# A graph layer and its experts: node gathers 1.5 batches earlier in POOL's order, the expert program a batch earlier

## The chip, the cores and the metric

The kernel runs on one core of a Trainium2 chip. The metric is device time in microseconds, the median over runs. Matmuls run on TensorE (PE), elementwise work on VectorE (DVE) and ScalarE (ACT), indirect DMAs (gathers) are issued by GpSimd (POOL), plain DMAs by SyncE (SP). Each engine works through its own instructions in order; semaphores join them.

## The reference

```python
def gat_conv(x, W, attn_l, attn_r, src, dst, n_nodes):      # twice, over the edges src -> dst
    feat = (x @ W).reshape(n_nodes, H, D)
    e = leaky_relu(el[src] + er[dst], 0.2)                  # el, er: feat dotted with attn_l, attn_r
    ex = exp(e - segment_max(e, dst)[dst])
    alpha = ex / segment_sum(ex, dst)[dst]
    return segment_sum(alpha * feat[src], dst)
...
xn = _layernorm(x, axis=-1)
x = x + gnn(xn) + linear_attention(xn)                      # 6250 nodes, 256 features, 106250 edges
h = _layernorm(x, axis=-1)
w = softmax(h @ Wr + br)                                    # 8 experts, every node through all
y = sum_e w[:, e] * (relu(bn(relu(bn(h @ W1[e])) @ W2[e])) @ Wo[e] + bo[e])
out = x + y
```

## The kernel before

Layer two of the graph network and the experts run in one pass (`edge_pass` with `Experts`). The edges, sorted by their target node, are cut into 13 groups (Q) of 4 batches (PB); a batch n has 16 steps j (G). At each step POOL gathers 128 rows of the table (L1349), ACT scales them (L1486) and DVE adds them to a running sum along each of 128 lanes, the ring (L1463). Three buffers (B) hold the rows, so POOL may be up to three batches ahead of DVE; it waits for `summed` of the batch three back. At step 6 of a batch DVE does the `head` of the next one (L1402 to L1421), which waits for all 16 gathers of that next batch. SP stores the sums of each half batch.

A node whose edges run over lanes or groups needs carries, the tails. For group q they are made in the first batch of the group after it (n = 4q + 4): ACT copies the last sums, then TensorE and DVE turn, scan (DVE step 3), shift (step 6), scale (step 8) and join (step 12, ending with L1191). SP then writes them to memory (`sync_out`, L1248 and L1250), with `tails.out` as their semaphore.

When group g is complete, its nodes (4 blocks of 121) go through the expert program. POOL gathers for each block its sums and its carries: 8 node gathers (`gather`, L1829), the first of which waits for the stores and for `tails.out`. In the order before they stand behind the first 8 edge gathers of batch 4(g + 2), one after each. DVE merges the two parts (`below`, `shares`, `join`), adds the residual, takes mean and variance (`spread`) and normalizes (`norm`, L1952 and L1955); TensorE transposes (`turn`, L2137), ACT copies (`turned`), TensorE forms the gate logits (`gate`, L2148) and runs the 8 experts: `first_layer` (L2097), `second_layer` (L2109), `outputs` (L2123), with ACT's `keep` (L2032) between them and DVE's `add_result` (L1885) behind. The order on each engine is written out by hand: on DVE, ACT and SP by batch and step (r = n // 4, kq = n % 4; f = r - 2 is the group whose experts run, g = r - 1 the one that is joined), on TensorE by the loop in `tensor` over r and the expert e, two experts for a batch. Batches beyond the 52nd exist only for the expert program (`vector_last`, `scalar_last`, `sync_last`), and the node gathers of the last two groups stand in `pool_last`.

Of the kernel before, what the change touches and what calls it, by code (L numbers as in the profile page):

```python
# [19 lines left out]
G = 16  # L20
T = NB * G
Q = 13
PB = NB // Q
J = T // Q
CAP = P * J
KB = NB // Q
# [3 lines left out]
E = 8  # L30
# [17 lines left out]
class Layer:  # L48


    def __init__(self, name, heads, width, act_heads, buffers, ahead):
        self.name, self.heads, self.width = name, heads, width
        self.buffers, self.ahead = buffers, ahead
        self.dim = width // heads
        self.table = width + 8
        self.row = width + 2 * heads
        self.den = width
        self.max = width + heads
        self.act_heads = act_heads
# [736 lines left out]
class Mixing:  # L796
# [263 lines left out]
    def pool(self, pool, n, j):  # L1060
        pass
# [636 lines left out]
class Experts:  # L1698
# [3 lines left out]


    LAST = (Q + 2) * PB

    def __init__(self, nc, a, k, s, tails, stored):
        self.nc, self.a, self.k, self.tails, self.stored = nc, a, k, tails, stored
# [57 lines left out]
    def valid(self, f):  # L1765
        return 0 <= f < Q


    def sync_first(self, sp):
        a = self.a  # L1770
# [30 lines left out]
                     self.y[:, f % 3, :, :]).then_inc(self.y_out, 16)  # L1801

    def sync(self, sp, n, half):
        r, kq = n // PB, n % PB
        if kq == 1 and half == 0 and self.valid(r - 3):
            self.store(sp, r - 3)
        if kq == 1 and half == 1 and self.valid(r - 1):
            self.load_rest(sp, r - 1)

    def sync_last(self, sp):  # L1810
        for n in range(NB, self.LAST + 3):
            self.sync(sp, n, 0)
# [19 lines left out]
                                     ).then_inc(self.rows_in[i], 16)  # L1832

    def pool(self, pool, n, j):
        if n % PB == 0 and n >= 2 * PB and j < 2 * KB:
            self.gather(pool, n // PB - 2, j // 2, j % 2)

    def pool_last(self, pool):
        for g in (Q - 2, Q - 1):
            for i in range(KB):  # L1840
                for j in range(2):
                    self.gather(pool, g, i, j)
# [140 lines left out]
        nc.vector.tensor_tensor(self.w[:, :, :], self.lge[:, :, :], broad(self.tot[:, :], E), ALU.mult).then_inc(self.w_ready, 1)  # L1983

    def vector(self, dve, n, j):
        r, kq = n // PB, n % PB
        f, g = r - 2, r - 1
        if j in (1, 2, 8, 9):
            o, e = (f, 2 * kq - 2) if kq else (r - 3, E - 2)
            if self.valid(o):  # L1990
                self.add_result(dve, o, e if j < 8 else e + 1, (j - 1) % 7)
        if self.valid(f):
            if kq == 0 and j == 3:
                self.gates(dve, f)
            if kq == 0 and j == 12:
                self.gate_shares(dve, f)
            if kq == 3 and j in (3, 4):
                self.add_bias(dve, f, j - 3)
        if not self.valid(g):
            return  # L2000
        if kq == 2:
            if j == 3:
                self.below(dve, g)
            if j == 7:
                self.shares(dve, g)
            if j in (7, 10, 11, 13):
                self.join(dve, g, (7, 10, 11, 13).index(j))
            if j == 14:
                self.spread(dve, g)
        if kq == 3 and j == 5:  # L2010
            self.norm(dve, g)

    def vector_last(self, dve):
        for n in range(NB, self.LAST + 3):
            for j in range(1, G):
# [33 lines left out]
        last.then_inc(self.xt_ready, 1)  # L2049

    def scalar(self, act, n, j):
        nc, r, kq = self.nc, n // PB, n % PB
        f, g = r - 2, r - 1
        if self.valid(f):
            if j == 2:
                self.keep(act, f, 2 * kq + 1, 0)
            if j == 5:
                self.keep(act, f, 2 * kq, 1)
            if kq == 0 and j == 7:
                act.wait_ge(self.lg_ready, f + 1)  # L2060
                wait(act, self.w_ready, f)
                nc.scalar.activation(self.lge[:, :, :], self.lg[:, :, :], ACT.Exp).then_inc(self.lge_ready, 1)
            if kq == 2 and j == 3:
                self.weights(act, f)
        if self.valid(g):
            if kq == 2 and j == 4:
                act.wait_ge(self.d_ready, g + 1)
                wait(act, self.joined, KB * g)
                nc.scalar.activation(self.sc[:, :, :], self.d[:, :, :], ACT.Exp).then_inc(self.sc_ready, 1)
            if kq == 3 and j == 3:  # L2070
                act.wait_ge(self.sd_asked, g + 1)
                nc.scalar.activation(self.sd[:, :], self.var[:, :], ACT.Sqrt).then_inc(self.sd_done, 1)
            if kq == 3 and j == 8:
                self.turned(act, g, 0)
                self.turned(act, g, 1)
        if self.valid(f):
            if kq < 3 and j == 9:
                self.keep(act, f, 2 * kq + 2, 0)
            if j == (12 if kq < 3 else 10):
                self.keep(act, f, 2 * kq + 1, 1)  # L2080
        if self.valid(g) and kq == 3 and j == 13:
            self.keep(act, g, 0, 0)

    def scalar_last(self, act):
        for n in range(NB, self.LAST + 3):
            for j in range(G):
# [81 lines left out]
    def tensor(self, pe):  # L2168
        tails = self.tails
        for r in range(Q + 3):  # L2170
            f, g, o, q = r - 2, r - 1, r - 3, r - 1
            on = self.valid(f)
            for e in range(E):
                if e == 7 and self.valid(g):
                    self.turn(pe, g)
                if on and e < E - 1:
                    self.first_layer(pe, f, e + 1)
                if e == 0 and self.valid(q):
                    tails.tensor_turn(pe, q)
                if e == 1 and self.valid(q):  # L2180
                    if on:
                        pe.wait_ge(self.lg_ready, f + 1)
                    tails.tensor_sum(pe, q)
                if e == 2 and 0 <= q < Q - 1:
                    tails.tensor_spread(pe, q)
                if e == 4 and on:
                    self.turn_weights(pe, f)
                if e == 5 and on:
                    self.bias(pe, f)
                if on:  # L2190
                    self.second_layer(pe, f, e)
                if e == 0 and self.valid(q):
                    tails.tensor_back(pe, q)
                if e == 7 and self.valid(g):
                    pe.wait_ge(self.xt_ready, 2 * (g + 1))
                    if g == 0:
                        for i in range(4):
                            pe.wait_ge(self.f1_in[i], 16)
                    self.first_layer(pe, g, 0)
                if e == 0 and self.valid(o):  # L2200
                    self.outputs(pe, o, E - 1)
                if e > 0 and on:
                    self.outputs(pe, f, e - 1)
                if e == 7 and self.valid(g):
                    self.gate(pe, g)


# [82 lines left out]
```

## Time and profile before

| | us |
|---|---|
| median of 3 runs (lowest, highest) | 3355.85 (3355.46, 3357.4) |
| the profiled execution's own time | 3355.96 |
| its span, first to last instruction | 3353.5 |
| layer two's first edge gather on POOL | 1925.7 |
| its last edge gather on POOL | 3122.65 |

The span is the profiled execution without the 2.5 us that lie around it; times of instructions are microseconds from the start of the span. "Idle before" in a row is the time in which the engine did nothing ahead of the row, with what released it; "issue" is a releaser that the profile doesn't show.

### The profile page before, as it was taken

What the parts mean: (1) busy time and instruction counts of PE and PEld (TensorE: products, weight loads), DVE (VectorE), ACT (ScalarE), POOL (GpSimd) and SP (SyncE); (2) the same over time, 40 slices, a digit from 0 to 9 for tenths busy, and PEclk for the clock granted to TensorE, in tenths of its full rate; (3) what the DMA queues carried; (4) which work ended last, traced back from release to release, by engine and by line L of the source; (5) the groups of instructions that cost most, each with busy time, mean ns of one, the idle gap of its engine ahead of it and who ended that gap; (6) DMA issues with size and microseconds to landing.
All of it is one profiled execution on the core that took longest, in us unless ns stands there. A gap on an engine that the chain in (4) does not pass through costs nothing. (4 is left out here: it accounts for less than half of the span.)

```text
span 3353.5 us, 33809 instructions
## 1 busy us (share of the span) xinstructions
PE 2061.7 (61%) x6977; PEld 1301.7 (39%) x6977; DVE 2423.0 (72%) x6006; ACT 1879.5 (56%) x6177; POOL 2147.9 (64%) x2067
## 2 busy tenths in 40 slices
PE   6800354455545544444456500389999999999999
PEld 5600233333323322332244300255555555555565
DVE  6881799999988888888778535566666676767632
ACT  3400687777877766676544322456566566656632
POOL 2326777767666767676277577777777777777300
PEclk9955666666665555555588855699999999999999
DMA  7512899999999999999665357666666666666400
GB/s 232 138 22 82 277 368 346 354 351 360 348 350 344 366 352 367 346 366 365 258 169 147 85 170 246 197 188 207 206 207 208 217 217 205 201 205 207 156 26 12
DMA packets 249060, 793.61 MB, mean 237 GB/s; under 512 B 72064, under 2 KB 120035, under 8 KB 222197
## 3 DMA queue, kind: packets, MB, share of 16 engines
q0 software_dynamic: 132448, 379.32, 36.3%
q1 hardware_dynamic: 86327, 391.15, 30.7%
q10 hardware_dynamic: 30078, 20.99, 2.5%
q8 instruction: 56, 0.92, 0.1%
q14 instruction: 151, 1.24, 0.1%
HBM read 414.03 MB, written 378.16 MB: 236 GB/s over the span
## 5 line engine op out<-in xcount | busy, mean ns | idle before, releaser
L1349 POOL DMA_INDIRECT e_rows<-scratch_table,k_src x1664 | 1716.4, 1031 | 643.9 <-issue 347.9
L1486 ACT ACTIVATE e_rows<-e_rows,e_wr 128x64 f32<-128x64 f32 (+1 forms) x4160 | 1186.2, 367 | 3.4
L1463 DVE SCALAR_TENSOR_TENSOR e_ring<-e_ring,e_kext,e_rows 128x512 f32<-128x512 f32 (+1 forms) x1560 | 958.8, 615 | 239.1 <-ACT e_rows L1486 151.1
L2123 PE MATMUL e_p_y<-e_wfo,e_h 128*121 128x256 f32 x1664 | 394.1, 392 | 41.4 <-DVE e_y L1885 41.3
L2123 PEld LDWEIGHTS e_p_y<-e_wfo,e_h 128*121 128x121 f32 x1664 | 314.5, 191 | 139.6 <-ACT e_h L2032 66.5
L2109 PE MATMUL e_p_b<-e_h,e_wf 128*128 128x484 f32 x832 | 359.7, 575 | 10.6 <-ACT e_h L2032 10.6
L2097 PE MATMUL e_p_a<-e_xt,e_wf 128*128 128x484 f32 x832 | 357.6, 573 | 0.7 <-ACT e_xt L2047 0.7
L2032 ACT ACTIVATE e_h<-e_p_a,e_shift,e_scale 128x484 f32<-128x484 f32 x208 | 155.3, 752 | 269.6 <-PE e_p_a L2097 269.6
L986 PE MATMUL e_p_c<-e_vext,e_kphi 121*128 121x129 f32 x208 | 63.9, 462 | 310.2 <-DVE e_kphi L878 310.2
L1885 DVE SCALAR_TENSOR_TENSOR e_y<-e_p_y,e_w,e_y 121x256 f32<-121x256 f32 x416 | 180.3, 475 | 102.4 <-PE e_p_y L2123 102.3
L1430 DVE TENSOR_TENSOR e_rows<-e_rows,e_shared 128x4096 f32<-128x4096 f32 x52 | 229.6, 4416 | 15.4 <-ACT e_wr L1479 15.4
L2109 PEld LDWEIGHTS e_p_b<-e_h,e_wf 128*128 128x128 f32 x832 | 154.3, 191 | 178.5 <-issue 171.3
L2097 PEld LDWEIGHTS e_p_a<-e_xt,e_wf 128*128 128x128 f32 x832 | 157.6, 191 | 146.4 <-issue 140.9
L1008 PE MATMUL e_p_q<-k_ident,e_low 121*128 121x121 f32 x104 | 34.5, 434 | 291.8 <-DVE e_low L906 291.8
L2032 ACT ACTIVATE e_h<-e_p_b,e_shift,e_scale 128x484 f32<-128x484 f32 x208 | 152.6, 749 | 87.9 <-PE e_p_b L2109 86.1
L975 PE MATMUL e_p_kv<-e_wkv,nd_feat 128*121 128x512 f32 x208 | 184.2, 1041 | 0.0
L986 PEld LDWEIGHTS e_p_c<-e_vext,e_kphi 121*128 121x128 f32 x208 | 48.5, 323 | 318.5 <-DVE e_kphi L878 318.5
L1008 PEld LDWEIGHTS e_p_q<-k_ident,e_low 121*128 121x128 f32 x104 | 16.2, 215 | 297.0 <-DVE e_low L906 297.0
L951 ACT COPY e_att_t<-e_p_q 128x242 f32<-128x242 f32 x52 | 18.8, 362 | 182.0 <-PE e_p_q L1008 182.0
L1682 PE MATMUL hi_p_f<-hi_w,hi_ht 128*121 128x272 f32 x416 | 120.2, 439 | 0.0
L1016 PE MATMUL e_p_c<-e_wproj,e_att_t 128*121 128x256 f32 x208 | 105.8, 662 | 18.1 <-ACT e_att_t L951 18.1
L218 POOL DMA_INDIRECT na_found<-in_dst,na_piece x52 | 54.8, 1054 | 94.7 <-DVE na_piece L270 94.7
(406 smaller groups left out, 3466.7 us busy)
## 6 DMA issues: line engine op xcount, KB each, us to landing
scratch_sums<-e_ring SPq DMA_DIRECT2D x104, 2112.0 KB
scratch_sums<-e_ring SPq DMA_DIRECT2D x104, 1032.0 KB
e_rows<-scratch_table,k_src POOLq DMA_INDIRECT x1664
scratch_table<-na_frow ACTq DMA_DIRECT2D x52, 245.8 KB
scratch_table<-hi_frow ACTq DMA_DIRECT2D x52, 124.8 KB
na_x<-in_x SPq DMA_DIRECT2D x13, 484.0 KB
e_wkv<-in_x SPq DMA_DIRECT2D x52, 121.0 KB
scratch_res<-e_wkv SPq DMA_DIRECT2D x52, 121.0 KB
```

Source lines behind the costliest of these rows:

```text
L975: nc.tensor.matmul(self.p_kv[0:BK, :], self.k.feat[:, t, kt, :], self.wkv[:, kt, :], start=kt == 0, stop=kt == 1)
L986: last = nc.tensor.matmul(self.p_c[:, m * (P + 1):(m + 1) * (P + 1)], self.kphi[:, m * P:(m + 1) * P], self.vext[:, m, :], start=False, st ...
L1349: nc.gpsimd.indirect_dma_start(out=rows[:, n % B, g, :], out_offset=None, in_=table, in_offset=bass.IndirectOffsetOnAxis(ap=k.src[:, n * G ...
L1430: c(nc.vector.tensor_tensor(v, v, broad(share(b)[:, AH:H, 1:G1].rearrange("p h j -> p j h"), dim), ALU.mult))
L1463: nc.vector.scalar_tensor_tensor(ring[:, i, j - c0, 0:W], prev, kext[:, 0, j + 1:j + 2], rows[:, rb, j, 0:W], ALU.mult, ALU.add).then_inc( ...
L1486: last = nc.scalar.activation(rows[:, rb, j, at], rows[:, rb, j, at], ACT.Copy, scale=wr[:, b, h, j + 1:j + 2])
L1682: last = nc.tensor.matmul(p_f[b][0:BK, 0:D + 16], ht[:, b, kt, :], w2[:, kt, :], start=kt == 0, stop=kt == 3)
L1885: last = nc.vector.scalar_tensor_tensor(y, self.p_y[bank][0:BK, i % 2 * D:(i % 2 + 1) * D], self.w[:, i, e:e + 1], y, ALU.mult, ALU.add)
L2032: self.nc.scalar.activation(h[:, e % 2, mt, :], p[mt][:, 0:GN], ACT.Relu, bias=self.shift[:, layer, 2 * e + mt:2 * e + mt + 1], scale=self ...
L2097: last = nc.tensor.matmul(self.p_a[mt][:, 0:GN], self.wf1[:, e, kt, mt * P:(mt + 1) * P], self.xt[:, kt, :], start=kt == 0, stop=kt == 1)
L2109: last = nc.tensor.matmul(self.p_b[mt][:, 0:GN], self.wf2[:, e, kt, mt * P:(mt + 1) * P], self.h1[:, e % 2, kt, :], start=kt == 0, stop=kt ...
L2123: last = nc.tensor.matmul(self.p_y[bank][0:BK, i * D:(i + 1) * D], self.h2[:, e % 2, kt, v:v + BK], self.wfo[:, e, kt, :], start=kt == 0, ...
```

## The change

The node gathers of group g are issued in batch 4g + 6 behind the last 8 edge gathers (steps 8 to 15), those of group 11 too, so that `pool_last` is left with group 12. On DVE, ACT and SP the expert program takes its place from n + 1 instead of n (`place`), a batch earlier; the join's parts go to later steps of that shifted program, so that `below` is at step 11 of what was batch 4g + 6 and is now batch 4g + 5, and the norm is at step 9 of the batch behind it. On TensorE the tails' parts stand two experts later in the loop, weights and bias one expert later; `turn` stands behind `second_layer` of expert 7 and `outputs` ahead of the next group's first layer. The tails on DVE and ACT keep their batch and step.

```diff
+    AHEAD = 1
...
+    def place(self, n):
+        return (n + self.AHEAD) // PB, (n + self.AHEAD) % PB
...
     def sync(self, sp, n, half):
-        r, kq = n // PB, n % PB
+        r, kq = self.place(n)
...
     def pool(self, pool, n, j):
-        if n % PB == 0 and n >= 2 * PB and j < 2 * KB:
-            self.gather(pool, n // PB - 2, j // 2, j % 2)
+        if n % PB == 2 and n >= PB and j >= G - 2 * KB:
+            at = j - (G - 2 * KB)
+            self.gather(pool, n // PB - 1, at // 2, at % 2)
 
     def pool_last(self, pool):
-        for g in (Q - 2, Q - 1):
+        for g in (Q - 1,):
...
     def vector(self, dve, n, j):
-        r, kq = n // PB, n % PB
+        r, kq = self.place(n)
...
         if kq == 2:
-            if j == 3:
+            if j == 11:
                 self.below(dve, g)
-            if j == 7:
+            if j == 14:
                 self.shares(dve, g)
-            if j in (7, 10, 11, 13):
-                self.join(dve, g, (7, 10, 11, 13).index(j))
-            if j == 14:
+        if kq == 3:
+            if j in (1, 2, 4, 5):
+                self.join(dve, g, (1, 2, 4, 5).index(j))
+            if j == 6:
                 self.spread(dve, g)
-        if kq == 3 and j == 5:
-            self.norm(dve, g)
+            if j == 9:
+                self.norm(dve, g)
...
     def scalar(self, act, n, j):
-        nc, r, kq = self.nc, n // PB, n % PB
+        nc, (r, kq) = self.nc, self.place(n)
         f, g = r - 2, r - 1
+        if self.valid(g - 1) and kq == 0 and j == 0:
+            self.keep(act, g - 1, 0, 0)
...
-            if kq == 2 and j == 3:
+            if kq == 2 and j == 10:
                 self.weights(act, f)
         if self.valid(g):
-            if kq == 2 and j == 4:
+            if kq == 2 and j == 12:
...
-            if kq == 3 and j == 3:
+            if kq == 3 and j == 7:
...
-            if kq == 3 and j == 8:
-                self.turned(act, g, 0)
-                self.turned(act, g, 1)
...
-        if self.valid(g) and kq == 3 and j == 13:
-            self.keep(act, g, 0, 0)
+        if self.valid(g) and kq == 3 and j == 12:
+            self.turned(act, g, 0)
+            self.turned(act, g, 1)
...
             for e in range(E):
-                if e == 7 and self.valid(g):
-                    self.turn(pe, g)
                 if on and e < E - 1:
                     self.first_layer(pe, f, e + 1)
-                if e == 0 and self.valid(q):
+                if e == 2 and self.valid(q):
                     tails.tensor_turn(pe, q)
-                if e == 1 and self.valid(q):
+                if e == 3 and self.valid(q):
...
                     tails.tensor_sum(pe, q)
-                if e == 2 and 0 <= q < Q - 1:
+                if e == 4 and 0 <= q < Q - 1:
                     tails.tensor_spread(pe, q)
-                if e == 4 and on:
+                if e == 5 and on:
                     self.turn_weights(pe, f)
-                if e == 5 and on:
+                if e == 6 and on:
                     self.bias(pe, f)
                 if on:
                     self.second_layer(pe, f, e)
-                if e == 0 and self.valid(q):
+                if e == 2 and self.valid(q):
                     tails.tensor_back(pe, q)
+                if e == 7 and self.valid(g):
+                    self.turn(pe, g)
+                if e == 0 and self.valid(o):
+                    self.outputs(pe, o, E - 1)
+                if e > 0 and on:
+                    self.outputs(pe, f, e - 1)
                 if e == 7 and self.valid(g):
...
                     self.first_layer(pe, g, 0)
-                if e == 0 and self.valid(o):
-                    self.outputs(pe, o, E - 1)
-                if e > 0 and on:
-                    self.outputs(pe, f, e - 1)
-                if e == 7 and self.valid(g):
                     self.gate(pe, g)
```

## Rows read from the trace of the kernel before

**Rows 1.** The page: engines' busy time, granted clock in 40 slices, chain that ended last.
```profile
PE 2061.7 (61%) x6977; PEld 1301.7 (39%) x6977; DVE 2423.0 (72%) x6006; ACT 1879.5 (56%) x6177; POOL 2147.9 (64%) x2067
...
PEclk9955666666665555555588855699999999999999
...
PE e_p_y L2123 7%; PE e_p_b L2109 7%; PE e_p_a L2097 7%; DVE e_ring L1463 2%; POOL e_rows L1349 2%; POOL e_grow L1829 2%; DMA e_grow<-scratch_tails_b,e_index 1%; DVE e_grow L1929 1%; ACT e_rows L1486 1%; PE e_p_w L2148 1%; DVE e_y L1885 1%; DVE e_y L1933 0%; DVE e_y L1935 0%; ACT e_h L2032 0%; PE e_p_w L2137 0%
```

**Rows 2.** Stretches: length, busy (instructions) of PE, PEld, DVE, ACT, POOL; PEclk, DMA share, GB/s.
```profile
2680.00:2773.00 93.00, 88.45 (x295) 52.85 (x294) 64.39 (x205) 56.29 (x129) 71.06 (x73) 0.98 0.68 210
...
2692.50:2695.90 3.40, 3.40 (x9) 2.59 (x9) 3.30 (x8) 1.74 (x7) 2.79 (x3) 0.50 1.00 383
...
3178.40:3263.90 85.50, 85.50 (x294) 51.66 (x294) 30.08 (x87) 28.52 (x43) 8.20 (x8) 1.00 0.10 29
```

**Rows 3.** Waits in layer two (2050 to 3353): us in total, times, longest.
```profile
DVE e_gm L1905 <- DMA e_grow<-scratch_tails_b,e_index: 136.5, 12, 29.2
...
POOL e_grow L1829 <- DMA scratch_tails_b<-e_tl: 62.3, 1, 62.3
POOL e_rows L1349 <- DVE e_ring L1463: 57.9, 190, 0.3
```

**Rows 4.** Timeline of POOL: three node gathers, the last edge gather.
```profile
2399.99 1.03 POOL L1829 DMA_INDIRECT e_grow<-scratch_tails_b,e_index  x1 [0.30 <-issue]
...
2663.80 1.03 POOL L1829 DMA_INDIRECT e_grow<-scratch_tails_b,e_index  x1 [0.31 <-issue]
...
3050.47 1.03 POOL L1829 DMA_INDIRECT e_grow<-scratch_tails_b,e_index  x1 [0.31 <-issue]
...
3122.65 0.95 POOL L1349 DMA_INDIRECT e_rows<-scratch_table,k_src  x1 [0.30 <-DVE e_ring L1463]
```

**Rows 5.** Timeline, batch 4: last gather of batch 5, its head, the carries' join.
```profile
2060.43 0.95 POOL L1349 DMA_INDIRECT e_rows<-scratch_table,k_src  x1 [0.30 <-issue]
...
2063.19 0.18 DVE L1402 TENSOR_TENSOR e_z<-e_rows,e_er 128x16 f32<-128x16 f32 x1 [6.63 <-DMA e_rows<-scratch_table,k_src]
...
2069.77 0.43 DVE L1191 TENSOR_TENSOR e_cr<-e_tl,e_ts 128x257 f32<-128x257 f32 x1
```

**Rows 6.** Timeline, batch 48: head, ACT's keep, the carries' join.
```profile
3099.14 0.17 DVE L1402 TENSOR_TENSOR e_z<-e_rows,e_er 128x16 f32<-128x16 f32 x1
...
3106.55 0.75 ACT L2032 ACTIVATE e_h<-e_p_a,e_shift,e_scale 128x484 f32<-128x484 f32 x1 [0.87 <-PE e_p_a L2097]
...
3109.89 0.50 DVE L1191 TENSOR_TENSOR e_cr<-e_tl,e_ts 128x257 f32<-128x257 f32 x1
```

**Rows 7.** Timeline, group 12: carries joined, POOL's first node gather.
```profile
3193.67 0.43 DVE L1191 TENSOR_TENSOR e_cr<-e_tl,e_ts 128x257 f32<-128x257 f32 x1
...
3196.98 1.02 POOL L1829 DMA_INDIRECT e_grow<-scratch_sums,e_index  x1 [62.31 <-DMA scratch_tails_b<-e_tl]
```

**Rows 8.** Timeline of DVE, group 6: head of batch 31, norm.
```profile
2685.44 0.17 DVE L1402 TENSOR_TENSOR e_z<-e_rows,e_er 128x16 f32<-128x16 f32 x1
...
2708.09 1.39 DVE L1955 TENSOR_SCALAR e_grow<-e_y,e_mv,e_rstd 121x256 f32<-121x256 f32 x4
```

**Rows 9.** Timeline of PE: outputs behind a wait; turn to expert 4, group 11.
```profile
2691.60 5.37 PE L2123 MATMUL e_p_y<-e_wfo,e_h 128*121 128x256 f32 x16 [2.74 <-DVE e_y L1885]
...
3166.08 0.58 PE L2137 MATMUL e_p_w<-k_ident,e_grow 121*128 121x121 f32 x4
...
3178.48 3.49 PE L2097 MATMUL e_p_a<-e_xt,e_wf 128*128 128x484 f32 x8
...
3192.21 0.59 PE L1171 MATMUL e_p_w<-e_ts,k_group 128*128 128x256 f32 x2
...
3196.11 3.62 PE L2123 MATMUL e_p_y<-e_wfo,e_h 128*121 128x256 f32 x16
...
3212.76 3.41 PE L2109 MATMUL e_p_b<-e_h,e_wf 128*128 128x484 f32 x8
```

## The prediction

> **What bounds the kernel now.** I read the page first: engine shares and the chain that ended last. No engine is busy throughout, and the chain ends in TensorE rows [rows 1]. The table by stretches separates two regimes. In a group in mid layer two TensorE is busy 88.45 of 93 us; in the last two groups it is busy 85.50 of 85.50 [rows 2]. So a group of the expert program costs TensorE 85.5 us, and before the end something slower paces it. The waits of layer two show a tempting stall: the vector engine (DVE) stands 136.5 us in twelve waits for the node gathers [rows 3]. POOL's own timeline shows why that stall is cheap now. POOL issues one gather after another with 0.30 us between them, and never stops for long in front of an edge gather (57.9 us in 190 waits of at most 0.3 us, the ordinary gap) [rows 3, 4]. From one group's last node gather to that of the seventh group after it POOL takes 3050.47 - 2399.99 = 650.5 us, 92.9 us a group: 64 edge and 8 node gathers [rows 4]. POOL is the pace in the middle, TensorE from the last edge gather (3122.65) on [rows 4]. Every wait of POOL itself therefore lengthens layer two one for one; a DVE wait does not.
>
> **What is neutral.** No arithmetic, gather or byte is added: 832 edge and 104 node gathers stay, the same matmuls, adds and activations. SP's store of a group's result and its load of the residual come one batch earlier, `store` before the first half's store of batch 4g+4 (its adds are done a batch before, so it holds nothing up) and `load_rest` behind `sync_out`. Both lie beside the stores and I cost them at 0. POOL passes no other queue work than its own edge gathers.
>
> **The gain, if nothing waits.** For group g the node gathers leave batch 4g+8, steps 0 to 7, for batch 4g+6, steps 8 to 15. Those of group 11 used to stand behind the last edge gather and now stand ahead of it, so the last edge gather ends 8 x (1.03 + 0.30) = 10.7 us later [rows 4]. Then the norm of group 11 stands 9.4 us after that end (worked out below), and from it to the first layer of its expert 1 TensorE needs the last turn, `outputs`, `first_layer` and `gate`: 0.3 + 3.5 + 3.2 + 1.6 = 8.6 us (steps of the kind shown in [rows 9]). Start of the last two groups: 3123.6 + 10.7 + 9.4 + 8.6 = 3152.3, against 3178.5 now [rows 9]: 26 us earlier. From there to the end the work is the same two groups of TensorE, so 26 us would be the whole gain. The DVE stalls of 11.4 us each (136.5 over 12) do not come off in each group, since POOL still needs its 92.9.
>
> **The new wait.** `gather(g)` waits for `tails.out`, the carries of group g. They come from step 12 of DVE's batch 4g+4. In the old order POOL asks for them one and a half batches later, so it waited only once, 62.3 us, behind the last edge gather, where it costs nothing [rows 3]. Now POOL asks nine edge gathers after the end of batch 4g+5: 9 x 1.28 + 0.3 = 11.9 us (the mean edge gather: 92.9 less 8 x 1.34, over 64). But DVE can't be early. At step 6 of batch 4g+4 it needs all rows of batch 4g+5 (`head`), and the best case, early in the layer, is 1.8 us from the last gather's end (2061.38) to that instruction (2063.19) [rows 5]. From there to the end of the carries it took 7.0 us with no experts running [rows 5] and 11.2 with them and TensorE late (3099.14 to 3110.39) [rows 6]. The tails' DMA then needs 2.9 us from 3194.10 to POOL's restart at 3196.98 [rows 7]; a second DMA issue behind it makes it 3.3. I call this the short circuit: 1.8 + (7.0 to 11.2) + 3.3 - 11.9 = a wait of 0.2 to 4.4 us in each group. With TensorE ahead and only DVE's own steps and adds, 9 us is the nearest value, so 2.2 us. Behind POOL's wait stand all following edge gathers, and behind these DVE, ScalarE and TensorE.
>
> The Trainium skill, "DMA: Bandwidth & Descriptors", in its anatomy of one DMA, gives a fixed 2.0 us and a term for the bytes, some 2.3 us for this table by its formula; the row says 2.9, and with 2.3 the wait would be 0.6 us shorter. That sentence can be left out.
>
> **The long circuit.** The wait may be longer, because DVE, ACT and TensorE must run a full loop between two POOL requests. I follow it from S, the start of the first node gather.
> 1. POOL alternates 8 node and 7 edge gathers; the last edge row ends at S + 18.1, `head` starts at S + 20.0 (1.3 and 1.25 us a piece [rows 4], landing 1.8 [rows 5]).
> 2. DVE, from this `head` to the end of the norm: now 2685.44 to 2709.48 = 24.0 us [rows 8]. The norm moves from step 5 to step 9: a second `head` (1.3), four ring steps (1.8), two adds (1.6) and some 0.5 for the square root: 29.2.
> 3. TensorE's `turn` needs the norm; a TensorE that has finished `second_layer` 7 stands there. From the turn to the end of the first layer of expert 4, behind which the join of the carries now lies: 3166.08 to 3212.76 = 46.7 in the old order, less the turn (0.8, overlapped; 0.3 stays), less `second_layer` 7 (3.3), which now precedes, and less `tensor_sum` (0.6), which now follows: 42.3 [rows 9].
> 4. ACT keeps expert 4's second half at DVE's step 9, before the rows of steps 10 and 11: from its start at 3106.55 to the end of the carries at 3110.39, 3.9 us [rows 6]. Then 3.3 for the DMA.
>
> Sum: 20.0 + 29.2 + 42.3 + 3.9 + 3.3 = 98.7 us a group, against 92.9: POOL waits 5.8. TensorE stands idle for several microseconds in two places of each loop. Now, after a wait of 2.7 us, a stretch of 3.4 us at granted clock 0.50 (the 1.2 GHz level) follows in a group [rows 2], and an `outputs` took 5.37 us where another took 3.62, 1.8 more [rows 9]. If this falls on the path behind the turn, 100.5 and a wait of 7.6.
>
> The Trainium skill, "TensorE: Matmul & The Clock Gate", Part 1, says that the array is throttled unless it is busy and falls back to half clock when it idles. The 0.50 stretch agrees. By this rule the idle TensorE here starts each loop at half clock, for the 7.6; without it 5.8.
>
> I take 6.5, between these two, nearer to the lower as the fall may come where TensorE has slack. Group 0 waits 0.6 us (carries end at 2070.20 [rows 5], POOL would ask at about 2073), group 1 only the short circuit (2.4), groups 2 to 11 ten times 6.5 = 65. Start of the last two groups: 3123.6 + 10.7 + 0.6 + 2.4 + 65 + (9.4 + 8.6) = 3220.3. The 9.4: S + 49.2 for the norm's end less S + 39.8 for the end of the next batch's gathers. Against 3178.5 that is 41.8 later. The last group's join needs no more cover than it has: its gathers should land some 52 us after that start, where TensorE is at expert 5, and its norm is done at about 76 of 85, just when `turn` asks. If this cover is lost it costs what the norm is late, 0 to 3 us.
>
> So the profiled execution goes from 3355.96 to about 3397.8. The median of the runs shown, 3355.85, is 0.1 below that time, so I predict **3397.7 us**.
>
> **The rivals.**
> - *Only the short circuit holds* (TensorE keeps far enough ahead). Eleven waits of 0.2 to 4.4 us: 26 us of gain less 2 to 49; with 2.2 each about no change, 3354; by the bounds 3333 to 3379. For it: DVE is busy only 64 of 93 us now, TensorE has 7 to idle [rows 2]. Against it: `turn` now stands behind `second_layer`, and the norm four steps later. Chance 0.2, of which a third is faster.
> - *No wait at POOL* (faster): the carries are out before POOL asks. 3355.85 - 26 = 3330. It decides at an average wait of 2.3 us, below which the change wins. It needs `head` to carries in under 6.8 us, and even the row without experts shows 7.0 [rows 5]. Chance 0.07.
> - *More than the sum*: half clock at both restarts, or ACT's table loads and keeps on the path: 8.5 to 10 us a group, 3418 to 3433. Chance 0.13.
> - *The long circuit as summed*, 5.8 to 7.6 us a group: 3391 to 3409. Chance 0.6.
> That the change does nothing has no case of its own: 26 us and the waits would have to cancel, which is the middle of the first rival.
>
> **Range and chances.** 3358 to 3424 takes in the long circuit, half of the short and half of the worse case: 0.8. The likeliest alone: 3388 to 3413. A difference under 0.2% (6.7 us) is no change. Faster: 0.07 + a small part of the short circuit = 0.11. Same: 0.06. Slower: 0.83.
>
> **What would show it.** Right: a wait of POOL at the node gathers (L1829 of now) on the tails' DMA in nearly each group, 5 to 8 us, where now it is one; node gathers 98 to 101 us apart; the DVE wait for node gathers (136.5) nearly gone and in its place a wait of `head` for edge rows, some 10 us a group; TensorE waiting for the norm before `turn` in most groups; the last edge gather at 3190 to 3215. The prediction is wrong if POOL stays gapless (then 3330), if the pitch is under 95.5, or if the last two groups take more than 85.5 each.

## The result: 2.2% slower, and the profile after

| | before | after |
|---|---|---|
| median (lowest, highest), 4 runs each | 3356.62 (3355.46, 3359.66) | 3431.41 (3429.05, 3434.17) |
| ratio, 95% interval | | 1.0223 (1.021 to 1.0235) |
| the profiled execution's own time, span | 3355.96, 3353.5 | 3434.17, 3431.6 |
| last edge gather on POOL starts | 3122.65 | 3234.12 |

Forecast were 3397.7 us, 42 more than before, in a range of 3358 to 3424. The sign was right; measured are 75 more, outside the range. In the experiments e1 to e12 every kernel ran slower than here and in e13 to e18, the kernel before by 8 to 9% (3629, 3635 and 3660 us) and the others by up to 15% (the kernel after 3903), one chip ran both ways, and no size is taken from those runs.

The page of the kernel after, the lines that answer to [rows 1]:

```profile
PE 2097.3 (61%) x6977; PEld 1331.5 (39%) x6977; DVE 2425.3 (71%) x6006; ACT 1884.5 (55%) x6177; POOL 2142.3 (62%) x2067
...
PEclk9855666666655555555588656999999999999999
...
PE e_p_y L2129 8%; PE e_p_a L2103 8%; PE e_p_b L2115 5%; POOL e_rows L1349 4%; DVE e_ring L1463 3%; POOL e_grow L1833 2%; DMA e_rows<-scratch_table,k_src 1%; DVE e_y L1890 1%; ACT e_rows L1486 1%; DVE e_grow L1934 1%; PE e_p_w L2154 1%; DVE e_y L1938 1%; DVE e_y L1940 1%; ACT e_h L2038 1%; PE e_p_w L2143 0%
```

The counts of instructions are those of before: no work was added. The busy times of DVE, ACT and POOL differ by less than 6 us. TensorE is busy 35.6 us longer for the same 6977 matmuls, at a mean granted clock of 0.744 instead of 0.752; it does no more work, so the 75 us are waiting and slower matmuls. The chain that ended last runs through POOL's edge gathers for 4% of the span, where it was 2%, and through DVE for 8% (5% before).

Stretches of the kernel after, in the order of [rows 2]: one group (from one first node gather to the next), three microseconds of the `outputs` behind a turn, and a stretch among the last two groups:

```profile
2478.00:2580.30 102.30, 91.06 (x295) 55.30 (x294) 64.76 (x206) 56.80 (x130) 69.96 (x73) 0.93 0.59 189
...
2530.00:2533.00 3.00, 3.00 (x9) 2.28 (x9) 2.43 (x6) 2.81 (x8) 2.39 (x3) 0.50 0.57 168
...
3259.00:3344.50 85.50, 85.50 (x293) 51.59 (x292) 35.78 (x100) 33.02 (x61) 8.22 (x8) 1.00 0.17 50
```

A group takes 102.3 us instead of 92.9. POOL is busy 69.96 us in it as in a group of before (71.06 in 93): it no longer sets the pace. Behind the turn the granted clock is 0.50, the 1.2 GHz level. The end of the layer is unchanged, TensorE without a gap.

Waits in layer two of the kernel after (2050 to 3432), to be read against [rows 3]:

```profile
DVE e_z L1402 <- DMA e_rows<-scratch_table,k_src: 181.6, 16, 17.7
...
PE e_p_w L2143 <- DVE e_grow L1960: 111.3, 12, 49.0
POOL e_grow L1833 <- DMA scratch_tails_b<-e_cr: 107.9, 12, 11.5
POOL e_grow L1833 <- DMA scratch_tails_b<-e_tl: 60.1, 1, 60.1
```

DVE's wait for node gathers (136.5 us) is gone. In its place POOL waits twelve times for the carries. Less the ordinary gap of 0.3 us, the first two waits are 1.3 and 2.3 us and the other ten 8.9 to 11.2, 10.1 on average. Behind POOL stand the edge gathers, and so DVE's `head` (181.6 us), and behind DVE the norm and TensorE's turn (62 us in eleven waits, the twelfth being the 49.0 of the last group).

One round of the loop in the kernel after, from the first node gather of group 4 to that of group 5, and the last edge gather (timeline of all engines):

```profile
2478.26 1.03 POOL L1833 DMA_INDIRECT e_grow<-scratch_sums,e_index  x1 [10.08 <-DMA scratch_tails_b<-e_cr]
...
2498.13 0.18 DVE L1402 TENSOR_TENSOR e_z<-e_rows,e_er 128x16 f32<-128x16 f32 x1 [13.20 <-DMA e_rows<-scratch_table,k_src]
...
2527.62 1.40 DVE L1960 TENSOR_SCALAR e_grow<-e_y,e_mv,e_rstd 121x256 f32<-121x256 f32 x4
...
2528.29 1.04 PE L2143 MATMUL e_p_w<-k_ident,e_grow 121*128 121x121 f32 x4 [5.65 <-DVE e_grow L1960]
...
2529.93 5.29 PE L2129 MATMUL e_p_y<-e_wfo,e_h 128*121 128x256 f32 x16
...
2570.30 3.41 PE L2103 MATMUL e_p_a<-e_xt,e_wf 128*128 128x484 f32 x8
...
2573.74 0.76 ACT L2038 ACTIVATE e_h<-e_p_a,e_shift,e_scale 128x484 f32<-128x484 f32 x1 [0.87 <-PE e_p_a L2103]
...
2577.09 0.43 DVE L1191 TENSOR_TENSOR e_cr<-e_tl,e_ts 128x257 f32<-128x257 f32 x1
...
2580.29 1.14 POOL L1833 DMA_INDIRECT e_grow<-scratch_sums,e_index  x1 [10.43 <-DMA scratch_tails_b<-e_cr]
...
3234.12 0.95 POOL L1349 DMA_INDIRECT e_rows<-scratch_table,k_src  x1 [0.30 <-DVE e_ring L1463]
```

| step of the long circuit | forecast | here |
|---|---|---|
| S to `head` of batch 4g+6 | 20.0 | 19.9 |
| to the norm's end | 29.2 | 30.9 |
| to the end of expert 4's first layer | 42.3 | 44.7 |
| to the carries | 3.9 | 3.8 |
| to the next S | 3.3 | 2.8 |
| sum | 98.7 | 102.0 |

### The profile page after: what moved, and what is told of

The parts are those of the page before. It is cut to its first block and busy times, and to the rows that moved or that the text cites. A ratio compares the mean times of both kernels' runs of the same rounds, so it can differ in the third digit from the quotient of the medians.

```text
span 3431.6 us, 33809 instructions
## 1 busy us (share of the span) xinstructions
PE 2097.3 (61%) x6977; PEld 1331.5 (39%) x6977; DVE 2425.3 (71%) x6006; ACT 1884.5 (55%) x6177; POOL 2142.3 (62%) x2067
## 3 DMA queue, kind: packets, MB, share of 16 engines
q0 software_dynamic: 132448, 379.32, 34.8%
## 5 line engine op out<-in xcount | busy, mean ns | idle before, releaser
L2129 PE MATMUL e_p_y<-e_wfo,e_h 128*121 128x256 f32 x1664 | 421.5, 411 | 64.9 <-DVE e_y L1890 64.9
L2129 PEld LDWEIGHTS e_p_y<-e_wfo,e_h 128*121 128x121 f32 x1664 | 334.3, 203 | 163.2 <-issue 88.5
L1402 DVE TENSOR_TENSOR e_z<-e_rows,e_er 128x128 f32<-128x128 f32 (+1 forms) x104 | 29.1, 280 | 254.0 <-DMA e_rows<-scratch_table,k_src 254.0
L1833 POOL DMA_INDIRECT e_grow<-scratch_sums,e_index x52 | 55.0, 1059 | 179.9 <-DMA scratch_tails_b<-e_cr 107.9
```

The source lines that it names most:

```text
L1833: nc.gpsimd.indirect_dma_start(out=self.rows[:, i, j, :], out_offset=None, in_=src, in_offset=bass.IndirectOffsetOnAxis(ap=self.index[:, 1 ...
L2129: last = nc.tensor.matmul(self.p_y[bank][0:BK, i * D:(i + 1) * D], self.h2[:, e % 2, kt, v:v + BK], self.wfo[:, e, kt, :], start=kt == 0, ...
```

## The experiments

**One table first.** For the kernels that ran at the usual 3356 us I read the same five stretches from the timelines, as means over the nine rounds that end at the node gathers of groups 3 to 11: a = S to `head` of 4g+6, b = to the norm's end, c = to the `head` of batch 4g+9 (two batches into the next group's experts), d = to the carries of g+1, e = to the next S. They add up to the distance of the groups.

| kernel | a | b | c | d | e | distance | POOL's wait |
|---|---|---|---|---|---|---|---|
| before | -5.2 | 53.4 | 18.7 | 11.2 | 14.7 | 92.9 | 0 |
| e17, POOL one batch forward | 3.7 | 51.6 | 18.4 | 11.2 | 8.4 | 93.4 | 0 |
| e18, POOL 1.5 batches forward | 19.8 | 45.7 | 19.2 | 11.2 | 3.0 | 98.9 | 5.5 |
| e16, the kernel after | 19.8 | 31.0 | 36.9 | 11.4 | 3.2 | 102.3 | 10.1 |
| e14, TensorE kept busy | 19.8 | 31.0 | 34.8 | 11.4 | 3.0 | 100.0 | 7.8 |
| e13, carries ahead of expert 4 | 19.9 | 31.0 | 36.7 | 6.1 | 4.0 | 97.8 | 5.4 |
| e15, both | 20.0 | 31.0 | 36.2 | 6.1 | 4.5 | 97.7 | 5.3 |

The shortest e that occurs is 2.8 to 3 us, the DMA of the carries. Where POOL doesn't wait for them, what e has beyond that is the slack of the loop: 11.7 us before, 5.4 in e17. In the other kernels POOL waits and there is none; what e13 and e15 have beyond 3 us is a slower DMA, not slack.

**e16, the kernel after once more**, beside e13 to e15: 3429.24 us (3425.63 to 3433.33), ratio 1.0215 (1.0197 to 1.0234). POOL waits 108.1 us for the carries, in twelve waits, as in the first profile (107.9).

**e18, POOL's new order alone** (e1 and e5 are the same kernel). The kernel before, with

```diff
-        if n % PB == 0 and n >= 2 * PB and j < 2 * KB:
-            self.gather(pool, n // PB - 2, j // 2, j % 2)
+        if n % PB == 2 and n >= PB and j >= G - 2 * KB:
+            at = j - (G - 2 * KB)
+            self.gather(pool, n // PB - 1, at // 2, at % 2)
 
     def pool_last(self, pool):
-        for g in (Q - 2, Q - 1):
+        for g in (Q - 1,):
```

> The kernel of e1 and e5: POOL's new order alone, the expert program where it was. Theory A: 18 from S to the end of batch 4g+6's gathers, 1.9, 53.5 to the norm's end, 29.6 to the carries, 3: 106 us a group, POOL waits about 13 us at each node gather, 3475 (ratio 1.035); so the shift of the program, which the kernel after has besides, earns back 4 us a group. Theory B: as the kernel after, 102 a group and 3431.

Measured 3413.16 us, ratio 1.0174 (1.0159 to 1.019). Its waits:

```profile
POOL e_grow L1829 <- DMA scratch_tails_b<-e_cr: 61.0, 12, 6.5
```

Neither number held. POOL waits less than in the kernel after, 98.9 us a group, not 106: I had taken b = 53.5 from the kernel before, but there DVE doesn't hurry; it is 45.7 when the loop binds. So in mid layer the program's shift, put on top of POOL's new order, earns nothing. It shortens b by 14.7 us and lengthens c by 17.7, as the experts that must be done before the carries are now two more. Of the 9.4 us a group that the change costs, 6.0 come with POOL's order and 3.4 more with the program's place. What the shift does earn stands behind the last edge gather: from that gather's end to the end of the span it is 213.6 us here and 196.6 in e16, 17 us less, while the last edge gather itself starts 34 us later in e16 (3225.57 against 3191.47).

**e17, one batch instead of a batch and a half** (e4 and e6 are the same kernel). As e18, but:

```diff
+        if n % PB == 3 and n >= PB and j < 2 * KB:
+            self.gather(pool, n // PB - 1, j // 2, j % 2)
```

> The kernel of e6: the kernel before with its node gathers one batch further forward instead of a batch and a half, the expert program where it was. Theory A (loop): from S to the norm's end 60, to the carries of the next group 29.6, to S' 3, 92.6 a group against POOL's own 92.9, so POOL waits 0 to 1 us a group. The last two groups' work begins one batch less late at the end of the layer. Time 3340 to 3356, ratio 0.995 to 1.0. Theory B (each batch that POOL asks earlier is paid in waits): about 5 us of wait a group, 3410.

Measured 3354.76 us against 3355.62, ratio 0.9989 (0.998 to 0.9998): less than the 0.2% that the prediction called no change. POOL's waits in layer two have no line for the carries of groups 0 to 11 any more; what is left at the node gathers is the ordinary gap:

```profile
POOL e_grow L1829 <- issue: 31.4, 103, 0.3
```

Theory A is right here (no wait, 93.4 us a group), theory B wrong. But nothing is gained at the end of the layer: the last edge gather starts at 3138.37 instead of 3122.65, 10.7 us of it for the eight node gathers now ahead of it and the rest from 93.4 against 92.9 over ten groups. What follows it is 17 us shorter (212.8 for 229.9), so the two nearly cancel; with the program unmoved the turn of group 11 stands at 3164.33, where it was 3166.08 [rows 9].

**e13, the carries ahead of expert 4** (e7 is the same kernel). The kernel after, on TensorE and at DVE's join:

```diff
             for e in range(E):
+                if e == 3 and self.valid(q):
+                    if on:
+                        pe.wait_ge(self.lg_ready, f + 1)
+                    tails.tensor_sum(pe, q)
                 if on and e < E - 1:
                     self.first_layer(pe, f, e + 1)
...
-                if e == 3 and self.valid(q):
-                    if on:
-                        pe.wait_ge(self.lg_ready, f + 1)
-                    tails.tensor_sum(pe, q)
...
-        if at == 12:
+        if at == (9 if self.L.width == 256 and self.L.heads == 1 else 12):
             self.vector_join(dve, q)
```

> The kernel of e7 (the kernel after with the carries' sums ahead of expert 4's first layer and DVE's join at step 9), now beside the kernel after (e16) on the same chip. Theory A (the loop through TensorE and the carries sets the distance of the groups): 5 us a group shorter than e16, as e7's 130.9 against e9's 136.1; 12 groups, 50 to 60 us faster than e16. Where the kernel before takes 3356: 3375 beside 3431. Theory D (POOL's asking order alone sets the wait): no difference.

Measured 3382.93 us, ratio 1.0076 (1.0059 to 1.0094): 46 us faster than e16, where 50 to 60 were forecast. Waits and two rows of its timeline:

```profile
POOL e_grow L1833 <- DMA scratch_tails_b<-e_cr: 58.0, 11, 6.3
```

```profile
2446.46 0.17 DVE L1402 TENSOR_TENSOR e_z<-e_rows,e_er 128x16 f32<-128x16 f32 x1
...
2452.13 0.43 DVE L1191 TENSOR_TENSOR e_cr<-e_tl,e_ts 128x257 f32<-128x257 f32 x1
```

`head` to carries is 6.1 instead of 11.4 us, and the distance falls by 4.5: 5.3 from d, 0.8 lost again in e. The carries now leave SP 3.1 to 3.2 us behind a store of half a batch's sums, in e16 8.2 to 8.5 us behind it. In these rounds e is 3.1 to 5.2 us in e13 and, but for one of 4.2, 2.8 to 3.3 in e16. SP's timeline for two rounds of e13, the first with an e of 3.7 us and the second with 5.2:

```profile
2449.49 0.32 SPq L1323 DMA_DIRECT2D scratch_sums<-e_ring  x1
2452.59 0.32 SPq L1248 DMA_DIRECT2D scratch_tails_b<-e_tl  x1
...
2545.86 0.34 SPq L1323 DMA_DIRECT2D scratch_sums<-e_ring  x1
2549.02 0.32 SPq L1248 DMA_DIRECT2D scratch_tails_b<-e_tl  x1
```

That the store so close ahead is what slows the carries is likely but not shown: it stands there in every round, also in those where e is 3.1.

Theory D, by which TensorE has no part in the wait, falls.

**e14, TensorE kept busy ahead of the turn** (e8 is the same kernel). It adds work that the reference has not:

```diff
+        if g >= 1:
+            pe.wait_ge(self.bias_added, 2 * (g - 1) + 1)
+            for i in range(6):
+                nc.tensor.matmul(self.p_u[0][:, 0:GN], self.wf1[:, 0, 0, 0:P], self.xt[:, 0, :], start=True, stop=True)
         for i in range(KB):
             pe.wait_ge(self.xn_ready, KB * g + i + 1)
```

> The kernel of e8 (the kernel after with six added matmuls in the gap ahead of the turn) beside e16. Theory A1 (the half clock behind the gap lies in the loop): 2 us a group shorter, some 25 us faster than e16; e8's 134.1 against e9's 136.1 fits. A2: no difference.

Measured 3409.6 us, ratio 1.0153 (1.0135 to 1.0171): 20 us faster than e16 (forecast were some 25), although TensorE does more.

```profile
2412.43 5.03 PE L2140 MATMUL e_p_w<-e_xt,e_wf 128*128 128x484 f32 x12
2418.08 0.78 PE L2147 MATMUL e_p_w<-k_ident,e_grow 121*128 121x121 f32 x4 [0.62 <-DVE e_grow L1960]
2418.75 0.75 PE L2147 MATMUL e_p_x<-k_ident,e_grow 121*128 121x121 f32 x4
2419.34 3.62 PE L2129 MATMUL e_p_y<-e_wfo,e_h 128*121 128x256 f32 x16
```

The six matmuls are twelve instructions in the trace. With the gap filled (0.62 us of it is left) the turn takes 0.78 and 0.75 instead of 1.04 and 1.01, and `outputs` 3.62 instead of 5.29; the granted clock is 1.00 over the whole stretch:

```profile
2409.20:2423.00 13.80, 13.18 (x46) 7.60 (x45) 12.67 (x41) 7.74 (x21) 10.45 (x12) 1.00 0.57 183
```

The half clock did lie in the loop: 2.3 us a group.

**e15, both.** The two diffs together.

> Both edits. Theory A with A1: they lie in one loop one behind the other, so the gains add: 7 us a group and some 80 us faster than e16; where the kernel before takes 3356, 3350. If only one of them binds, the larger of the two gains.

Measured 3381.6 us, ratio 1.0068 (1.0051 to 1.0085): no faster than e13. Here the gains don't add. Two rows show part of it, the turn of group 3 and the `outputs` behind it:

```profile
2411.48 1.07 PE L2147 MATMUL e_p_w<-k_ident,e_grow 121*128 121x121 f32 x4 [2.88 <-DVE e_grow L1960]
...
2413.14 4.22 PE L2129 MATMUL e_p_y<-e_wfo,e_h 128*121 128x256 f32 x16
```

With the carries moved the gap ahead of the turn is longer (in e13 7.5 us on average over eleven waits, in the kernel after 5.7), so six matmuls no longer fill it. TensorE still waits 2.4 us for the norm behind them (26 us over eleven waits), where it waits 0.9 in e14. The turn takes 1.07 us, as behind the open gap, and `outputs` 4.22, between the 3.62 of the full clock and the 5.29 behind the open gap. c gains 0.5 us and e loses 0.5. Why no more of the 2.3 us came stays open, and a fuller cover was not tried.

**e1 to e12**, at the slower pace named above; ratios are to the kernel before as run beside them. Their forecasts were worked out from the usual pace. Those for e1, e3 and e4 failed for the loop theory and for its rival alike, as each of these kernels lost more than either gave; e17 and e18 decide for e4 and e1, and e3 has no run at the usual pace.

e1, the kernel of e18: ratio 1.0773 (1.0709 to 1.0837); e5, again, 1.0743.

> Only POOL's order is changed: the node gathers stand in batch 4g+6, steps 8 to 15, and the expert program keeps its old place on the other engines. Loop theory (the wait is the closed loop gathers of g, join, norm, turn, the expert program up to where the carries of g+1 are joined, gathers of g+1, and the program's shift against the tails is what lengthened it): here the loop is 20 to the head, some 15 to the merge, 55.5 from the merge to the carries (2683.6 to 2739.1 in the kernel before) and 3, about 93.5; the short circuit then decides with 2 to 4.4 us a group. Node gathers 95 to 97 us apart, 3376 to 3396 us. Rival (POOL simply asks one and a half batches too early, whatever the program does): POOL waits about 10 us in each group as in the changed kernel, 102 apart, 3425 to 3435 us.

e2, the change without its part in `pool` and `pool_last`:

```diff
-        if n % PB == 2 and n >= PB and j >= G - 2 * KB:
...
+        if n % PB == 0 and n >= 2 * PB and j < 2 * KB:
+            self.gather(pool, n // PB - 2, j // 2, j % 2)
...
```

> Only the expert program is shifted a batch forward with its new order; POOL's node gathers stay at batch 4g+8, steps 0 to 7, and those of the last two groups at the end. Loop theory: from the merge of group g to the carries of g+1 it is 74 us (25.7 to the norm, 44.5 and 4.0 behind it in the changed kernel); POOL, with three buffers, is then held by DVE's sums at step 12 of batch 4g+11 and needs some 29 us from there to the landing of the next node gathers, so about 102 us a group, now as waits at edge gathers for the sums, and 3430 to 3460 us. Rival (early request): POOL asks late enough and never waits, 93 a group, 3345 to 3360 us.

Ratio 1.0005 (0.998 to 1.0031), no wait of POOL for the carries at the node gathers of groups 0 to 11. The loop theory forecast 3430 to 3460 us, a ratio of 1.022 or more, and was wrong here; the rival's 3345 to 3360 fits. So at this pace the program's place costs nothing while POOL asks late, and the 3.4 us a group of e18's comparison hold only on top of POOL's new order. It earns nothing at the end either: from the last edge gather on it is 230.0 us, the 229.9 of before. It is the only run of this part by itself, and there is none at the usual pace.

e3, the change with its node gathers at `n % PB == 3`, steps 0 to 7 (half a batch later than the change has them):

> The changed kernel with the node gathers half a batch later, at batch 4g+7, steps 0 to 7. POOL then asks 7 edge gathers, some 9 us, later; its wait was 9.9 us. Loop theory: the request's place is not what counts; the loop loses only the 3 us that the merge stood behind the landing (25.1 from the first node gather to the merge, 22 where nothing else holds it), so 99 us a group, a wait of about 6 us stays, 3397 to 3412 us. Rival (early request): the wait is all but gone, 93 to 94 a group, 3330 to 3345 us.

Ratio 1.0486 (1.0427 to 1.0545), between e2 and the kernel after (e9, 1.0659).

e4, the kernel of e17: 1.039 (1.033 to 1.045); e6, again, 1.0398. At this pace POOL waits for the carries even with one batch (e4, layer two), so that e17's "no change" holds for the usual pace only:

```profile
POOL e_grow L1829 <- DMA scratch_tails_b<-e_cr: 213.0, 12, 19.3
```

> The kernel before with only the node gathers moved, by one batch, to batch 4g+7, steps 0 to 7 (those of group 11 thus ahead of the last edge gathers). Loop theory: the loop is about 80 and the carries are out some 5 us before POOL asks, so no wait of POOL, 92.9 a group; the DVE wait for node gathers goes; the norm of the last but one group comes some 5 us earlier, so 3346 to 3354 us. Rival (any earlier place costs, in proportion): a third of the way less cost than the changed kernel, some 5 us a group, 3385 to 3410 us.

e7 and e8, the kernels of e13 and e14: 1.0576 (1.0534 to 1.0618) and 1.0642 (1.0599 to 1.0684). e9, the kernel after: 1.0659 (1.0638 to 1.068). The order of the three is that of e13, e14 and e16.

> The kernel after, with the sums of the carries ahead of expert 4's first layer on TensorE, and DVE's join of the carries at step 9 of batch 4g+4 instead of 12, so that it no longer stands behind ACT's read of expert 4's first layer. Theory A (the loop norm, turn, experts 1 to 4, carries, node gathers sets 102.3 us a group): the loop is some 5 us shorter (the second layer of expert 2 ends 7 us ahead of the first layer of expert 4, less 2 for the steps between), POOL's wait falls from 9.9 to about 5 us a group, and the time from 3431 to about 3375 (ratio to the kernel before about 1.006). Theory B (the wait is DVE's own lateness, its adds and merges, whatever TensorE does in between): the wait falls by at most the 1.5 us of DVE's three steps, 3415. Theory C (landing of the node gathers or of the carries' DMA): no change, 3431.

> The kernel after, with six matmuls of 484 columns on TensorE in the gap ahead of each turn, which write a bank that the turn overwrites (work that the reference has not). They fill 4.9 us of the 5.65 in which TensorE waits for the norm, so that the clock should not fall to half ahead of the turn. Theory A1 (the half clock behind the gap is part of the loop): turn and output products 5.3 + 2.0 fall to 3.6 + 1.1, the loop is about 2.3 us shorter, POOL's wait 7.6 instead of 9.9, the time 3405. Theory A2 (the half clock runs beside something longer): no change, 3431. If the added matmuls end behind the norm, the loop grows by what they overrun.

> The kernel after as it is, for a comparison on the chip of this call. If the kernel before takes its 3356 us here, 3431. If it takes 3630 as in the eight runs so far: Theory A (the loop through TensorE sets the distance of the groups, and whatever makes TensorE's results late lengthens it) gives a ratio well above 1.022, as e7 and e8 had 1.058 and 1.064; e7 (carries ahead of expert 4) should be faster than this kernel by some 5 us a group, 50 in all, so about 3895, and e8 should be within 25 us of it. Theory D (only the asking order of POOL costs, by an amount that doesn't hang on TensorE) gives 1.022, 3710.

e10 (the kernel before), e11 (after) and e12 (e7) with two more waits on POOL in each batch of layer two:

```diff
+                    if L is L2 and n and g == 0:
+                        pool.wait_ge(rows_in[(n - 1) % B], ((n - 1) // B + 1) * 16 * G)
+                    if L is L2 and g == 8:
+                        pool.wait_ge(rows_in[n % B], n // B * 16 * G + 16 * 8)
                     wait(pool, summed, (n - B) * G + g + 1)
```

> The kernel before, with two added waits a batch in layer two: POOL asks for the first and the ninth edge gather of a batch only when the eight before it have landed, so that it pauses some 1.5 us eight times a group. In the profiles of e1 to e8 TensorE's results reach ACT up to 34 us late, always while POOL issues 30 or more gathers without a break, and the delay ends 5 to 7 us after POOL pauses. Theory H (gap-free issuing by POOL holds TensorE's results back on these chips): the delays over 10 us vanish, the distance of the groups is 92.9 + 8 x 1.3 = 103 instead of 113, and the time falls from 3630 to about 3520, although POOL is made to wait. Theory J (TensorE is slow there for another reason, the long runs of POOL are only its effect): the delays stay, 3630 or up to 100 more. On a chip on which the kernel before takes 3356 the pauses are a plain loss: about 3480.

> The kernel after with the same pauses. Theory A with H: without the delays the loop is the 102.3 us seen in the kernel after on the first chip; POOL's own work with the pauses is 103, so both meet: 103 to 105 a group and about 3530 where the kernel before takes 3630, and POOL's wait at the node gathers falls to 0 to 3 us. Theory J: no faster than e9. On a chip on which the kernel before takes 3356: POOL's wait of 9.9 us takes up the pauses, so it costs at most a few us a group, 3435 to 3465.

> e7 (the kernel after with the carries' sums ahead of expert 4 and DVE's join at step 9) with the same pauses. Theory A with H: the loop is 97 us and POOL with its pauses the bound, 103 a group: no wait at the node gathers, and the time that of e10 less the 26 us that the tail of the layer gains, about 3495 where e10 is 3520. Theory J: as e7.

Ratios 1.0066 (1.0039 to 1.0093), 1.0039 (1.0012 to 1.0065) and 1.0117 (1.0093 to 1.014). Theory H is wrong for e10, which got slower and not 110 us faster: the longest of ACT's waits for TensorE's late results is 10.9 us in it, against 38.5 in e9, and still the groups are some 113 us apart and not 103. e11 is 227 us faster than e9 (3675.91 against 3903.39), which theory J did not allow, but it stays above the kernel before, where H had it 100 us below; e12 is no faster than e10, where H had it 25 us ahead. So neither theory stands, and what made these runs long stays open.

## Where the prediction was right, and which step failed

*The reading of before* held. POOL set the pace in mid layer and TensorE at the end: in the kernel after, TensorE is still busy 85.50 of 85.50 us in a stretch of the last two groups.

*The gain at the end and the tail* held within 3.5 us. From the last edge gather's end to the end of the span I had 3397.8 - 2.5 - 3202.3 = 193.0 us; it is 3431.6 - 3235.1 = 196.5, where before has 229.9. The profiled execution exceeds the forecast 3397.8 by 36.4 us, and 32.8 of them stand at the last edge gather.

*The new wait and its place* held, and that the short circuit doesn't bind in mid layer. Group 1, for which only that was taken, waits 2.3 us (forecast 2.4), group 0 1.3 (0.6). The signs named under "What would show it" came in kind and missed in size: POOL's waits are 8.9 to 11.2 us and not 5 to 8, the node gathers 102.4 apart and not 98 to 101, `head`'s wait 13 to 15 from group 1 on and not some 10, the last edge gather at 3234 and not 3190 to 3215. None of the signs of being wrong came.

*What failed is the size of the long circuit*, the 6.5 us taken for the wait of groups 2 to 11. It is 10.1. The third rival, "more than the sum", had this size (8.5 to 10 us, 3418 to 3433) and a chance of 0.13. Two terms and a choice were too low:

1. Step 2, `head` to the norm's end: 29.2 taken, 30.9 measured. Grouped lines of DVE over this stretch, first after, then before (the 24.0 us that the term was built on):

```profile
L1463 DVE SCALAR_TENSOR_TENSOR e_ring<-e_ring,e_kext,e_rows 128x256 f32<-128x256 f32 x19 | 9.1, 478 | 1.6 <-ACT e_rows L1486 1.0
L1890 DVE SCALAR_TENSOR_TENSOR e_y<-e_p_y,e_w,e_y 121x256 f32<-121x256 f32 x12 | 5.2, 474 | 0.0
...
L1374 DVE TENSOR_TENSOR_SCAN e_er<-k_same,e_er 128x64 f32<-128x64 f32 x1 | 0.3, 291 | 0.0
```

```profile
L1463 DVE SCALAR_TENSOR_TENSOR e_ring<-e_ring,e_kext,e_rows 128x256 f32<-128x256 f32 x16 | 7.6, 476 | 0.3
L1885 DVE SCALAR_TENSOR_TENSOR e_y<-e_p_y,e_w,e_y 121x256 f32<-121x256 f32 x8 | 3.5, 474 | 0.0
```

Of the four ring steps that I counted three are there (16 to 19), and the adds are there (8 to 12). Not counted were 1.0 us in which DVE waits for ACT's rows, the scan of the next group's `er` (0.3 and its copy), and `below`, which now stands behind this `head` and not ahead of it.

2. Step 3, the norm's end to expert 4: 42.3 taken, 44.7 measured. In this term `outputs` was 3.62 us and the turn's rest 0.3; they are 5.29 and 0.9, at a granted clock of 0.50 behind a gap of 5.65 us. I had seen the half clock and put 1.8 us on it, for the upper bound only.

3. The choice of 6.5 between 5.8 and 7.6, "nearer to the lower as the fall may come where TensorE has slack". It did not. By the row of TensorE standing in front of the turn, the gap lies just ahead of the steps that the loop needs next; e14 removes it and gets 2.3 us back. The Trainium skill, "TensorE: Matmul & The Clock Gate", Part 1, had it that an idle array restarts at half clock; the rows agree here (`outputs` 5.29 against 3.62).

With both terms, 98.7 + 1.7 + 2.4 = 102.8 for a measured 102.0 to 102.3, the last 0.5 being the DMA of the carries, 2.8 instead of 3.3 us. The distance of the groups is 102.4 on average instead of 92.9 + 6.5 = 99.4: ten times 3.0 us are 30 of the 32.8.

What the prediction did not see at all is in the table: in mid layer two parts of the change work against each other. The carries stay with the edges, the experts move a batch forward, and so from e18 to e16 c grows by more than b shrinks. I had costed the loop only for the whole change, never for its parts.

One slip in the chances: "faster" got 0.11, but by the rivals' own figures it is 0.07 and a third of 0.2, some 0.14.

## What to carry to other kernels

When a request is moved forward in a queue, write down the closed loop from the request to the next one and compare its length with the pace of the engine that bounds the kernel: the slack of that loop (here 11.7 us of 92.9), not the length of a stall elsewhere, says by how much the loop may grow. That growth is not the distance moved. One batch forward, 16 edge gathers or some 20 us of POOL's order (an estimate from 1.28 us each), used only 6.3 us of the slack: DVE waits 50.9 us for the node gathers instead of 136.5, and from S to the norm's end it is 55.3 us instead of 48.2. The next half batch, some 10 us, used all of the 5.4 left and made 5.5 of wait. So price each place, not a rate. A stall on an engine that doesn't set the pace, like DVE's 136.5 us, is no gain to be had. Where a loop goes through TensorE and TensorE waits in it, price the step behind the wait at the slow clock from the start.

## What was not expected of the hardware

Added work made the kernel faster: six matmuls more in each turn (5.03 us in the row above) took 20 us off the kernel after, as the turn and `outputs` behind them then ran at a granted clock of 1.00. And matmuls behind a gap were slow for longer than the turn alone: 16 matmuls of `outputs` took 5.29 us behind a wait of 5.65, 4.22 behind one of 2.88 in e15, and 3.62 behind 0.62 in e14. The DMA of the carries took 2.8 to 3.3 us from DVE's last write to POOL's next instruction in most of the nine rounds of the kernel after and of e16, with one of 4.2 in each, but 3.1 to 5.5 in e13 and e15. The Trainium skill, "DMA: Bandwidth & Descriptors", in its anatomy of one DMA, gives a fixed 2.0 us and the bytes for a DMA that GpSimd issues, which makes an estimate of 2.3 us for this table. The carries' DMA is issued by SP, so that figure was not one for this DMA; the prediction took its terms from its own rows and doesn't rest on it.
